# Distances from raw rows with ScalarE's running sums, a comparison row in PSUM, and group sums in two banks

## The reference, cut to what matters

```python
x = x + gnn(layernorm(x), r, W, y, edge_index)
x = x + ffn(layernorm(x)[None], ...)[0]          # 8 experts, top 1

# gnn:
mems2 = mems.at[yi].set(r[0])
keep_w = (edge_index[1] != yi)
d2 = jnp.sum(jnp.square(mems2 - r), axis=-1)     # distance of every node to r
_, nbr = jax.lax.top_k(-d2, 7)                   # 7 more edges, into node yi
deg = segment_sum(w, col) + 2.0
dinv = rsqrt(deg)
msg = (dinv[row] * w * dinv[col])[:, None] * (mems2 @ W)[row]
out = segment_sum(msg, col) + (2.0 * dinv * dinv)[:, None] * (mems2 @ W)
```

## Time and profile before

| | us |
|---|---|
| median of 3 runs (2577.97 to 2581.65) | 2580.05 |
| the profiled execution's own time | 2580.54 |
| its span, first to last instruction | 2578.7 |
| first stage: start to the first gather of L669 | 245.58 |
| second stage: to the end of the last gather | 1555.08 |
| third stage, to the end | 778.04 |

### The profile page before, as it was taken

One profiled execution on the slowest core, in us unless ns is written; L12 is line 12 of the kernel. 1 busy time (PEld: TensorE's weight loads), 2 busy tenths in 40 slices (PEclk: granted clock), 3 DMA queues, 4 the chain that ended last, 5 costly groups with the idle time before them and its releaser, 6 DMA issues. The chain is left out here.

```text
span 2578.7 us, 36702 instructions
## 1 busy us (share of the span) xinstructions
PE 1961.2 (76%) x11096; PEld 1693.5 (66%) x11096; DVE 1325.4 (51%) x3782; ACT 1011.2 (39%) x1769; POOL 1542.0 (60%) x1612
## 2 busy tenths in 40 slices
PE   2002777976786696786878889998599999999995
PEld 1002655755675585574767778888588788788875
DVE  7969875155325425325243258787544354454443
ACT  1377655345425535425333233433233323322332
POOL 6631677777777777777777777777123422422234
PEclk8555888987898898898999989999699999999998
DMA  9226333743473474473655778877422212212121
GB/s 266 65 59 181 118 103 108 258 145 104 148 256 108 121 256 132 149 248 111 215 191 184 225 216 225 221 217 173 127 57 71 83 36 71 77 36 71 41 69 29
DMA packets 235521, 359.05 MB, mean 139 GB/s; under 512 B 46584, under 2 KB 172696, under 8 KB 235220
## 3 DMA queue, kind: packets, MB, share of 16 engines
q0 software_dynamic: 74176, 194.10, 26.1%
q1 hardware_dynamic: 159860, 160.86, 20.4%
q10 hardware_dynamic: 1312, 2.10, 0.3%
HBM read 305.38 MB, written 56.40 MB: 140 GB/s over the span
## 5 line engine op out<-in xcount | busy, mean ns | idle before, releaser
L669 POOL DMA_INDIRECT arena<-z_table,arena x1216 | 1179.2, 970 | 462.6 <-issue 357.4
L1790 PE MATMUL bank<-arena 128*128 128x128 f32 x4864 | 706.4, 306 | 273.1 <-DMA arena<-z_table,arena 153.4
L1790 PEld LDWEIGHTS bank<-arena 128*128 128x128 f32 x4864 | 657.6, 217 | 370.4 <-issue 298.0
L1254 DVE TENSOR_TENSOR nodes<-nodes,bank 128x256 f32 x304 | 127.8, 421 | 746.0 <-PE bank L1790 730.1
L729 POOL DMA_INDIRECT out<-arena x128 | 130.4, 1019 | 410.3 <-DVE arena L1668 389.7
L2031 PE MATMUL bank<-arena 128*128 128x256 f32 (+1 forms) x1472 | 329.5, 383 | 9.3 <-DVE arena L1616 9.3
L933 ACT ACTIVATE nodes<-bank,arena 128x256 f32<-128x256 f32 (+1 forms) x368 | 152.4, 465 | 451.8 <-PE bank L2031 451.8
L2043 PE MATMUL bank<-arena,nodes 128*128 128x256 f32 (+1 forms) x1472 | 326.0, 379 | 0.0
L2031 PEld LDWEIGHTS bank<-arena 128*128 128x128 f32 x1472 | 282.1, 195 | 50.2 <-DVE arena L1616 11.9
L817 ACT ACTIVATE arena<-iota_h,arena 128x490 f16<-128x490 f16 x280 | 194.7, 695 | 303.7 <-PE bank L1802 303.3
L2043 PEld LDWEIGHTS bank<-arena,nodes 128*128 128x128 f32 (+1 forms) x1472 | 272.7, 188 | 40.0 <-issue 1.0
(11 more groups left out here) (316 smaller groups left out, 1869.9 us busy)
## 6 DMA issues: line engine op xcount, KB each, us to landing
arena<-z_table SPq DMA_DIRECT2D x96, 768.0 KB, 4.4
arena<-z_table,arena POOLq DMA_INDIRECT x1216
arena<-in_L_ffn_w SPq DMA_DIRECT2D x14, 1024.0 KB, 8.2
z_table<-nodes SPq DMA_DIRECT2D x14, 896.0 KB, 6.7
x_rows<-nodes SPq DMA_DIRECT2D x98, 128.0 KB
arena<-in_x SPq DMA_DIRECT2D x48, 256.0 KB, 3.5
out<-nodes SPq DMA_DIRECT2D x96, 128.0 KB
nodes<-in_x SPq DMA_DIRECT2D x12, 896.0 KB, 11.5
```

The source lines that it names most:

```text
L669: nc.gpsimd.indirect_dma_start(gath[:, slot, t, :], None, z_table, bass.IndirectOffsetOnAxis(ap=src_idx[:, tile_at:tile_at + 1], axis=0)). ...
L1790: last = nc.tensor.matmul(agg_bank[i][:, k * P:(k + 1) * P], gath[:, i, t, k * P:(k + 1) * P], sel[:, i, t, :], start=(t == 0), stop=(t == ...
```

## The change

The distance is taken from the raw rows: with s = 1/sigma and t = -mean/sigma of a node, `mems2 - r` is (s x - r) + t. VectorE's `far_rows` (one instruction per window) makes s x - r into a ring of FR = 16 windows; ScalarE's `far_square` adds t, squares, and gives the sum over the window's 256 features by its accumulator (98 Squares). The table row is x times `far_scale` = dinv s plus `far_shift` = dinv t, one multiply-add per window: chunks 1 and 6 on ScalarE, chunks 0, 2, 3, 4, 5 on VectorE. Nothing is normalised in place any more, `differ`, `sum_squares` and the multiplication by `dinv` go, and `far_rows` and the squares of 64 windows no longer follow `dinv`. The work on limits is cut into pieces that stand between the pieces of `far_rows`; the limits are reduced straight from PSUM, and the test of order between rows is done on 128 partitions.

`select` and the low half of the strips compare with `count_up`, a copy of 0..127 in PSUM bank 7, in place of `iota_b` in SBUF. The sums have two banks, AB = 2.

```diff
-    AB = 4
+    AB = 2
...
-    ACT_WIN = 40
-    EARLY = 9
+    EARLY = 7
+    FR = 16
+    Z_ACT = (1, 6)
+    Z_DVE = [c for c in range(NZC) if c not in Z_ACT]
+    SQ_EACH, SQ_MID = 10, 4
+    FAR_TO = [16, 30, 46, 60, 76, NW]
...
-        agg_bank = [bank[0], bank[1], bank[6], bank[7]]
+        agg_bank = [bank[0], bank[1]]
+        count_up = bank[7][:, 0:P]
...
-            pool.wait_ge(S["dist_ok"], 2 * NZC)
+            pool.wait_ge(S["square_ok"], NW)
...
+            def far_square(w):
+                act.wait_ge(S["diff_ok"], w + 1)
+                nc.scalar.activation(diff[:, w % FR, :, :], diff[:, w % FR, :, :], ACT.Square, bias=shift[:, w:w + 1],
+                                     accum_out=dist[:, w:w + 1]).then_inc(S["square_ok"], 1)
+
+            def scale_chunk(c):
+                act.wait_ge(S["diff_ok"], (c + 1) * ZC)
+                for w in range(c * ZC, (c + 1) * ZC):
+                    nc.scalar.activation(node_row(w), node_row(w), ACT.Identity, bias=far_shift[:, w:w + 1],
+                                         scale=far_scale[:, w:w + 1]).then_inc(S["z_act"], 1)
...
             for b in range(EARLY, 2 * NZC):
-                for w in range((b - EARLY) * part, min((b - EARLY + 1) * part, ACT_WIN)):
-                    normalise(w)
                 count_first(b)
+                here_from = (b - EARLY) * SQ_EACH
+                for w in range(here_from, here_from + (SQ_EACH if b < 2 * NZC - 1 else SQ_MID)):
+                    far_square(w)
...
-            for w in range(ACT_WIN, NW):
-                nc.vector.tensor_scalar(nodes[:, :, w, :], nodes[:, :, w, :], rstd[:, w:w + 1], shift[:, w:w + 1],
-                                        ALU.mult, ALU.add).then_inc(S["mem_ok"], 1)
...
+            def far_rows(first, last):
+
+                for w in range(first, last):
+                    if w >= FR:
+                        dve.wait_ge(S["square_ok"], w - FR + 1)
+                    nc.vector.scalar_tensor_tensor(diff[:, w % FR, :, :], nodes[:, :, w, :], rstd[:, w:w + 1],
+                                                   r_rows[:, :].rearrange("p (k c) -> p k c", k=KD),
+                                                   ALU.mult, ALU.subtract).then_inc(S["diff_ok"], 1)
...
+            far_rows(0, FAR_TO[0])
+            group_limits()
+            far_rows(FAR_TO[0], FAR_TO[1])
+            unit_limits()
+            far_rows(FAR_TO[1], FAR_TO[2])
+            spread_limits()
+            far_rows(FAR_TO[2], FAR_TO[3])
+            set_keys()
+            far_rows(FAR_TO[3], FAR_TO[4])
...
+            for c in Z_DVE:
+                if c == Z_DVE[-1]:
+                    far_rows(FAR_TO[4], FAR_TO[5])
+                scale_chunk(c)
...
             def select(step):
                 t0 = (DG + step) * GT
-                nc.vector.tensor_tensor(sel[:, step % SR, :, :], iota_b[:, :].unsqueeze(1).to_broadcast([P, GT, P]),
+                nc.vector.tensor_tensor(sel[:, step % SR, :, :], count_up.unsqueeze(1).to_broadcast([P, GT, P]),
                                         rel_b[:, t0:t0 + GT].unsqueeze(2).to_broadcast([P, GT, P]),
                                         ALU.is_equal).then_inc(S["sel_ok"], 1)
...
-                    last = nc.vector.tensor_scalar(oh_low[:, n % 2, t, :], iota_b[:, :], low_h[:, tile:tile + 1], None, ALU.is_equal)
+                    last = nc.vector.tensor_scalar(oh_low[:, n % 2, t, :], count_up, low_h[:, tile:tile + 1], None, ALU.is_equal)
...
+            nc.tensor.matmul(count_up, ident[:, :], iota_r[:, :], start=True, stop=True).then_inc(S["count_up_ps"], 1)
```

More of the change, by code:

```diff
@@ L410, in build @@
         mine_y = sb("mine_y", [P, 1])
+        not_mine = sb("not_mine", [P, 1])
+        row_cross = sb("row_cross", [P, EB])
+        far_scale, far_shift = pos_lo, pos_hi
         r_y = sb("r_y", [P, D])
@@ L1071, in _ @@
+            then(nc.vector.tensor_reduce(cross_sum[:, :], row_cross[:, :], AX.X, ALU.add))
+            then(nc.vector.tensor_tensor(disorder[:, :], disorder[:, :], cross_sum[:, :], ALU.add))
             dve.wait_ge(S["r_in"], 16)
@@ new lines, in unit_limits @@
+            def unit_limits():
+                then(nc.vector.tensor_scalar(unit_cmp, unit_lo, TOP_BASE, None, ALU.min))
+                for p in range(NP):
+                    mine, start = slice(UNIT0[p], UNIT0[p + 1]), unit_cmp[0:1, UNIT0[p]:UNIT0[p] + 1]
+                    then(nc.vector.tensor_copy(unit_bad[0:1, mine], start.to_broadcast([1, UNITS[p]])))
+                    then(nc.vector.tensor_copy(piece_i[0:1, p:p + 1], start))
+                then(nc.vector.tensor_tensor(unit_rel, unit_cmp, unit_bad, ALU.subtract))
+                for mine, top in ((slice(0, TWOS), P - PANEL - 1), (slice(TWOS, UN), P - PANEL)):
+                    then(nc.vector.tensor_scalar(unit_rel[0:1, mine], unit_rel[0:1, mine], float(top), 0.0, ALU.min, ALU.max))
+                then(nc.vector.tensor_tensor(unit_abs, unit_rel, unit_bad, ALU.add))
+                then(nc.vector.tensor_tensor(unit_dif, unit_hi, unit_abs, ALU.subtract))
+                then(nc.vector.tensor_scalar(unit_bad, unit_dif, float(PANEL), None, ALU.is_ge))
@@ L1177, in _, with scale_chunk @@
             then(nc.vector.tensor_scalar(gap2[:, :], gap2[:, :], -0.5, 1.5, ALU.mult, ALU.add))
[L1178 to L1195 removed]
+            then(nc.vector.tensor_tensor(dinv[:, :], dinv[:, :], gap2[:, :], ALU.mult))
+            then(nc.vector.tensor_tensor(far_scale[:, :], dinv[:, :], rstd[:, :], ALU.mult))
+            then(nc.vector.tensor_tensor(far_shift[:, :], dinv[:, :], shift[:, :], ALU.mult))
+            dve.sem_inc(S["deg_ok"], 1)
+            def scale_chunk(c):
+                dve.wait_ge(S["diff_ok"], (c + 1) * ZC)
+                for w in range(c * ZC, (c + 1) * ZC):
+                    last = nc.vector.tensor_scalar(nodes[:, :, w, :], nodes[:, :, w, :], far_scale[:, w:w + 1], far_shift[:, w:w + 1],
+                                                   ALU.mult, ALU.add)
+                last.then_inc(S["z_ok"], 1)
+            for c in Z_DVE:
+                if c == Z_DVE[-1]:
+                    far_rows(FAR_TO[4], FAR_TO[5])
+                scale_chunk(c)
             for w in range(0, NW, 2):
```

280 lines of the change are left out of this document (122 added, 158 removed).

## The result

The changed kernel takes 2516.78 us (median of 4 runs, 2514.71 to 2518.99) beside 2579.01 for the kernel before; the ratio is 0.9759, with an interval of 0.9742 to 0.9776. The forecast was 2521, with a range of 2509 to 2536. The profiled execution took 2514.71 with a span of 2513.2, which is 65.5 us under the span of before.

The account below looks back on a forecast made before the run. POOL's own pace of 1.248 us a gather was taken to bound the stream. From 2580.5: -28.8 (first stage), -26.5 (comparison row), -5 (start), +1 (two banks) gave 2521 us, with a range of 2509 to 2536.

Parts of the forecast that it names:

- What bounds the stream: Second stage: POOL moves at its own pace, 0.946 + 0.302 = 1.248 us a gather, 1517.6 of 1555.1 us.
- The comparison row, -26.5: Second stage: `select` with its comparison row in PSUM no longer holds gathers, -26.5 us, at most 29.2.
- The degrees, -6.0: First stage: POOL's 8.34 us stall on ScalarE's counts goes, -8.0, against +2.0 for `far_rows`; last count 6.0 us earlier.
- its second term: First stage: `far_rows` with two SBUF inputs, 0.34 us each, holds about 20 edge rows by 0.1, +2.0 us, bounds 0 and 7.
- Squares at 0.50: First stage, ScalarE: a square with its sum takes 0.50 us, its read hidden; 7.7 us a batch against POOL's 8.7.
- The rival with 0.77: First stage: squares take 0.77 us, nothing hidden, 10.4 us a batch against 8.7; total 2533 us; chance 0.08.
- The table, -28.8: End of first stage: first store at 169.2, fourteen transfers 3.23 us apart, first gather at 216.8 against 245.58, -28.8 us.
- that rival: End of first stage: stores don't keep 284 GB/s over fourteen, 6.5 us more, total 2527 us; chance 0.14.
- The start, -5: Start of the stream: sums ready nearly when POOL has its 16 gathers out, -5 of the 6 us, bounds 0 and -6.
- Two banks, +1: Second stage: TensorE's sum waits for VectorE's addition two steps back; tight only in the 68 node steps, +1 us.
- The rival of the node steps: Last 68 steps of the stream: TensorE becomes the bound and logits bite, some 8 us, total 2529; chance 0.07.
- the slower one: Node steps: two banks tie TensorE to VectorE, the two run in turn, total at or above 2581 us; chance 0.04.

Follow-up runs that it names:

- experiment 9: Kernel before with EARLY = 10 in place of 9, so ScalarE counts one more batch ahead of the root of the variances: 2574.64 us, ratio 0.9979.
- experiment 5: Changed kernel with `r` as a second row in PSUM, so that `far_rows` has one SBUF input: 2514.25 us, ratio 0.9736.
- experiment 1: Changed kernel with the comparison row back in SBUF for `select` alone: 2544.79 us, ratio 0.9869.
- experiment 4: Changed kernel with one bank for the sums in place of two (AB = 1): 2655.92 us, ratio 1.0298.
- experiment 6: Changed kernel with three long VectorE instructions with two SBUF inputs cut in four: 2516.76 us, ratio 0.9745.
- experiment 8: Changed kernel with the last 22 `far_rows` ahead of chunk 2's table rows in place of chunk 5's: 2523.58 us, ratio 0.9772.
- experiment 11: Changed kernel once more, unedited: 2516.66 us, ratio 0.9757.
- experiment 3: Kernel before with two banks for the sums in place of four and nothing else: 2578.91 us, ratio 0.9992.
- experiment 7: Changed kernel with `r` in PSUM for `far_rows` and three long VectorE instructions cut in four: 2512.16 us, ratio 0.9748.

## Why the prediction was right, point by point

- **What bounds the stream: right.** POOL's own pace set it, and now sets all of it: from one gather's start to the next it is 1.251 us at the median (the prediction had 1.248, with a gap of 0.302 us that is 357.4/1173 = 0.305) and 1.2506 at the mean, and no gap between two gathers is over 0.32 us.
- **The comparison row, -26.5: right, the size 2.4 short.** 1179.2 - 1150.3 = 28.9 us went; the little that I had left to the strips and other forms went too.
- **The degrees, -6.0: right as a sum (-6.5), by some luck, its second term mis-sized.** The stall was worth 8.0 (experiment 9). `far_rows` was put at +2.0; it cost 3.8 (23 edge rows, 0.165 each; 4.3 by experiment 5; 4.6 to 5.0 in experiments 1, 4, 6, 8 and 11), first because one takes 0.43 and not 0.34, then because a run of them held one gather for 1.13 (in those experiments 1.92 to 2.31). The prediction priced each gather by one instruction, and its sign of holds of up to 0.3 did not hold. The sum came out right since I had not counted what goes: the normalisations (L1106), which stood there before, had held ten edge rows by 1.3 us, and a long operation on limits (L1066) one by 1.0. All edge rows together: 102.4 us against 101.0.
- **Squares at 0.50: right, 0.49.** The read of the sum hides, as with the counts. A batch takes 7 x 0.387 + 10 x 0.492 = 7.6 us, and ScalarE waits 1.4 to 2.7 us for edge rows in each of the batches behind the first squares. The rival with 0.77 is out.
- **The table, -28.8: right (-28.9).** First store 168.66 (169.2 forecast), first gather 216.67 (216.8); in experiments 4 and 11, with the same first stage and the longer hold, 217.6. The stores keep their 3.2 us over all fourteen, so that rival is out; experiment 8 shows that they lose time only where the queue is empty.
- **The start, -5: right, all 6 went.** The sums were ready 1.6 us ahead of need.
- **Two banks, +1: 0** (experiment 3). The rival of the node steps is out, and the slower one, which needs one bank to appear (experiment 4).
- **The rest.** The stream's 34.7 us are 4.2 more than the 30.5 of the sum (2.4 gathers, 1 start, 1 banks), and the profiled execution's other 1.9 lie in the untouched stage, so that the runs' median, 2516.78, is nearer to the forecast than the profiled run.

## What to carry to other kernels

Where POOL issues indirect DMAs back to back, look at the mean of a gather beside its median: a mean above it says that something holds some of them, and the instruction that VectorE runs 0.1 us after their start names it. An operand that never changes can be moved to PSUM, if a bank can be spared, and banks can be spared where the traces show microseconds between an addition and the next use of its bank; ask what stands last in that bank's step before going from two to one. Where a queue of transfers sets a stage's end, what counts is that it never runs empty from its first transfer on, so the work ahead of the first one is worth its full time and the rest only what the queue misses.

## What the runs showed of the hardware beyond that

A gather held by VectorE can stay held through a run of back-to-back instructions with two SBUF inputs (1.13 us over three of them, 1.92 over five, 2.31 over six), and not only to the end of the one it met (0.33); what decides between the two was not tried. The start does not tell: of the gathers that began 8 to 20 ns behind the start of a `far_rows`, some lost nothing, some were held by that one instruction, and some by the rest of the run.

An instruction with two SBUF inputs is not the only one that holds a gather. A normalisation of the kernel before (L1106) reads one tensor and two columns of scalars from SBUF, and ten edge rows got through only when the one they started in had ended:

```profile
132.78 0.40 DVE L1106 TENSOR_SCALAR nodes<-nodes,columns 128x256 f32<-128x256 f32 x1
133.05 1.08 POOL L654 DMA_INDIRECT arena<-dst_rows,first_i  x1 [0.30 <-issue]
```

Other forms with one tensor from SBUF hold nothing: `bn_stats` of the same width and, in experiment 5, `far_rows` with `r` in PSUM met some 25 edge rows each, at 0 ns each. What sets these apart was not tried, so a form is best judged by the gathers that meet it.

And the same gathers take a median of 946 ns in most profiled executions and 949 in others (experiments 7 and 8), with 1.254 us from one to the next in place of 1.251, which makes 3.6 us over 1216 of them; what sets that was not tried.
